# A gated cross-attention and expert-mix block: a quarter of the mix is added by GpSimd, with the engine orders laid out anew

## What is computed

```python
x = x + tanh(g_xattn) * xattn(layernorm(x), ctx, mask, Wq, bq, ..., Wo, bo)   # windows of 128 columns, 8 heads of 32
x = x + tanh(g_ffn)   * ffn(layernorm(x), router_weight, router_bias, expert_bias)

def ffn(h, ...):                              # h: rows by 2048
    scores = softmax(h @ router_weight.T + router_bias)        # 64 experts
    w = the 8 largest scores of a row, zero elsewhere          # rows by 64
    return h * w.sum(-1) + w @ expert_bias                     # the mix
```

## Time and profile before

| | |
|---|---|
| runs | 1418.84 us median of 3 (1418.77 to 1421.61) |
| profiled execution | 1415.67 us, span of the core 1413.9 us |
| TensorE busy | 1294.0 us, 92% of the span |
| VectorE busy | 1090.5 us, 77% |
| GpSimd busy | 1012.6 us, 72% |
| ScalarE busy | 794.7 us, 56% |
| DMA | 124.67 MB, mean 88 GB/s |
| chain of work that ended last | TensorE 70%, VectorE 19%, ScalarE 5%, issue 4%, GpSimd 1% |

### The profile page before, as it was taken

The page is one execution under the profiler, slowest core; times in us unless marked ns, Lnnn a source line. Parts: engine busy times, 40 slices in busy tenths (PEclk is TensorE's granted clock), DMA queues, the critical chain, the costliest instruction groups (busy, mean ns, idle before and its releaser), DMA issues.

```text
span 1413.9 us, 39778 instructions
## 1 busy us (share of the span) xinstructions
PE 1294.0 (92%) x16064; PEld 1158.8 (82%) x16064; DVE 1090.5 (77%) x1949; ACT 794.7 (56%) x1430; POOL 1012.6 (72%) x988
## 2 busy tenths in 40 slices
PE   1899999899989999899998999989998999989964
PEld 1898998789978899689986899878997889869953
DVE  6569668896679867897778966889677986786665
ACT  1455665655565566655556556665556555666534
POOL 4487887578867788578885788757885788856650
PEclk9999999999999999999999999999999999999976
DMA  8431111541127111361114511163112611132003
GB/s 251 114 107 46 41 44 43 180 131 43 42 65 242 48 40 46 118 188 47 44 40 136 173 47 41 41 209 100 48 45 83 216 47 47 46 122 59 23 5 119
DMA packets 129269, 124.67 MB, mean 88 GB/s; under 512 B 12352, under 2 KB 97472, under 8 KB 128448
## 3 DMA queue, kind: packets, MB, share of 16 engines
q1 hardware_dynamic: 129088, 122.14, 28.7%
HBM read 88.45 MB, written 33.65 MB: 86 GB/s over the span
## 4 chain that ended last, share of the span: by engine, by line
PE 70%; DVE 19%; ACT 5%; issue 4%; POOL 1%; DMA 1%; SPq 0%; DVEq 0%; ACTq 0%; POOLq 0%
PE ring L279 7%; PE ring L280 7%; PE ring L281 7%; PE ring L348 4%; PE ring L387 4%; DVE X L859 4%; PE ring L319 4%; PE ring L357 4%; PE ring L388 4%; PE ring L294 4%; PE ring L389 4%; PE ring L295 4%; PE ring L296 4%; PE ring L400 4%; PE ring L371 3%
## 5 line engine op out<-in xcount | busy, mean ns | idle before, releaser
L279 PE MATMUL ring<-z_hi,wqk_hi 128*128 128x256 f32 x1024 | 291.8, 285 | 30.0 <-POOL z_lo L986 30.0
L280 PE MATMUL ring<-z_hi,wqk_lo 128*128 128x256 f32 x1024 | 290.8, 284 | 0.0
L281 PE MATMUL ring<-z_lo,wqk_hi 128*128 128x256 f32 x1024 | 290.6, 284 | 0.0
L1002 POOL TENSOR_TENSOR X<-X,xt 128x512 f32<-128x512 f32 x128 | 165.7, 1300 | 145.7 <-DVE xt L764 140.6
L1018 POOL TENSOR_SCALAR hc<-X,ln 128x256 f32<-128x256 f32 x256 | 233.3, 928 | 0.5 <-POOL X L1002 0.5
L764 DVE SCALAR_TENSOR_TENSOR xt<-ring,cst,mg 128x256 f32<-128x256 f32 x256 | 112.1, 479 | 151.8 <-PE ring L389 151.8
L591 ACT ACTIVATE q<-ring,cst 128x256 f32<-128x256 f32 x64 | 30.3, 474 | 350.3 <-PE ring L281 350.3
L279 PEld LDWEIGHTS ring<-z_hi,wqk_hi 128*128 128x128 f32 x1024 | 197.2, 193 | 33.1 <-issue 30.6
L748 DVE RECIPROCAL o<-ring 128x512 f32<-128x512 f32 x64 | 214.3, 3348 | 0.5 <-PE ring L357 0.5
L992 POOL TENSOR_TENSOR cx_lo<-cx,cx_hi 128x512 fp32r<-128x512 f32 x128 | 168.6, 1317 | 48.6 <-ACT cx_hi L599 48.6
L280 PEld LDWEIGHTS ring<-z_hi,wqk_lo 128*128 128x128 f32 x1024 | 197.4, 193 | 2.5
(11 more groups left out here) (131 smaller groups left out, 3366.4 us busy)
## 6 DMA issues: line engine op xcount, KB each, us to landing
cx<-in_ctx SPq DMA_DIRECT2D x128, 256.0 KB, 2.9
out_y<-X SPq DMA_DIRECT2D x128, 256.0 KB, 2.7
X<-in_x SPq DMA_DIRECT2D x112, 256.0 KB, 5.8
mk<-in_mask SPq DMA_DIRECT2D x64, 128.0 KB, 3.2
mg<-in_mask SPq DMA_DIRECT2D x64, 128.0 KB, 3.2
X<-in_x SPq DMA_DIRECT2D x4, 1024.0 KB, 8.0
sel<-rows_d SPq DMA_DIRECT2D x256, 3.0 KB
X<-in_eb SPq DMA_DIRECT2D x2, 512.0 KB, 8.1
```

The lines of the kernel that those rows point to most:

```text
L279: e.matmul(o, wqk_hi[:, t, cols], z_hi[:, t, :], t == 0, False)
L280: e.matmul(o, wqk_lo[:, t, cols], z_hi[:, t, :], False, False)
L281: last = e.matmul(o, wqk_hi[:, t, cols], z_lo[:, t, :], False, t == DT - 1)
```

## The change

The first of the four column blocks of a row tile, `c = 0`, is now added by GpSimd. ScalarE writes it into a buffer of its own, `xp`, instead of `xm`. GpSimd multiplies the four tiles of X with `c = 0` by the row's scale in one go (`scale_x`, 4 instructions, once the scale is there and the statistics have read X), and later adds `xp` to each (`add_mix`). VectorE keeps the other 12 additions. `xp` is one buffer, so ScalarE waits for GpSimd's addition of the row tile before. The stores of a row tile go in the order c = 1, 2, 3, 0. The slots of all engines are new.

```diff
-    rows=-10.75, z32=-26, z_hi=-16.75, z_lo=-14.25, q=-11, q_ev=-9, k=-9, k_ev=-3.75, mk=-33.5, mkb=-25,
-    c_hi=-15, c_lo=-10.5, v=-10.5, v_ev=-7.25, v_gap=-0.75,
-    S=0.75, top=2.5, split=6, MT=9, mt_ev=8.75, ST=14.25, exp=16.5, DEN=18.25, PV=18.5, rc=19, on=21.25,
-    gelu=24.25, mg=5, ot_hi=24.75, ot_lo=29, WO=30.25, WO_gap=1.5, xt=32.25, x1=35.5, bn2=40,
-    h=39.5, hT=43.25, hT_gap=0.25, ht_hi=45.25, ht_lo=44.75, R=51.25,
-    norm2=29.5, L=34.75, LT=35.5, c_top=35, c_exp=36, c_w=42, wT=41.75, wt_hi=43.75, wt_lo=42.75, mix=45.25, m_gap=0.25,
-    m_ev=47.5, x2=47.25, rl=52.5, rl_gap=1,
-    x_1=0.5, x_gap=3.75, bn1=64.75, bn1_gap=1.25, norm1=95,
+    rows=-10.75, z32=-26, z_hi=-16.75, z_lo=-14.25, q=-10.25, q_ev=-8.25, k=-8.25, k_ev=-3, mk=-33.5, mkb=-25,
+    c_hi=-14.25, c_lo=-10.25, v=-9.75, v_ev=-6.5, v_gap=-0.75,
+    S=1.25, top=3.25, split=6.75, MT=9.75, mt_ev=10.5, ST=15, exp=17.25, DEN=19, PV=19.25, rc=19.75, on=22,
+    gelu=25, mg=5, ot_hi=28.5, ot_lo=29.75, WO=31, WO_gap=1.75, xt=33, x1=36.25, bn2=39.75,
+    h=40, hT=44, hT_gap=0.25, ht_hi=47, ht_lo=45.5, R=52,
+    norm2=30.25, L=36.25, LT=36.25, c_top=35.75, c_exp=36.75, c_w=42.75, wT=42.5, wt_hi=44.5, wt_lo=43.5, mix=46, m_gap=0.25,
+    sx=47.25, m_ev=48.25, x2=48.25, rl=56.5, rl_gap=1,
+    x_1=0.5, x_gap=3.75, bn1=68.75, bn1_gap=1.25, norm1=95,
...
+        xp = sb("xp", [128, 512])
...
             def store(b, t, c):
-                e.wait_ge(x2_v, (b * DT + t) * 4 + c + 1)
+                if c == 0:
+                    e.wait_ge(x2_g, b * DT + t + 1)
+                else:
+                    e.wait_ge(x2_v, (b * DT + t) * 3 + c)
...
-                        store(b, i // 4, i % 4)
+                        store(b, i // 4, (i + 1) % 4)
...
             def shift_mix(b, t, c):
                 i = (b * DT + t) * 4 + c
-                if i >= 2:
-                    e.wait_ge(x2_v, i - 1)
+                n = (b * DT + t) * 3 + c - 1
+                if c == 0 and i:
+                    e.wait_ge(x2_g, b * DT + t)
+                elif c and n >= 2:
+                    e.wait_ge(x2_v, n - 1)
                 e.wait_ge(mix_pe, i + 1)
                 if t == 0 and c == 0:
                     e.wait_ge(ac_v, b + 1)
-                e.activation(xm[i % 2][:], bank("mix", i)[:], ACT.Identity, bias=sc[:, t, 7:8]).then_inc(xm_a, 1)
+                to = xm[n % 2] if c else xp
+                e.activation(to[:], bank("mix", i)[:], ACT.Identity, bias=sc[:, t, 7:8]).then_inc(xm_a, 1)
...
                     for b in batch(t, C["x2"] + C["m_gap"] * i):
-                        add_mix(b, i // 4, i % 4)
+                        if i % 4:
+                            add_mix(b, i // 4, i % 4)
...
+            def add_mix(b, t):
+                xs = X[b % 2][:, t, 0:512]
+                e.wait_ge(sx_g, DT * b + t + 1)
+                e.wait_ge(xm_a, (b * DT + t) * 4 + 1)
+                e.tensor_tensor(xs, xs, xp[:], ALU.add).then_inc(x2_g, 1)
+
+            def scale_x(b):
+                e.wait_ge(bn2_v, 16 * (b + 1))
+                e.wait_ge(ac_v, b + 1)
+                for t in range(DT):
+                    xs = X[b % 2][:, t, 0:512]
+                    e.tensor_scalar(xs, xs, sc[:, t, 6:7], None, ALU.mult).then_inc(sx_g, 1)
...
+                for b in batch(t, C["sx"]):
+                    scale_x(b)
+                for k in range(DT):
+                    for b in batch(t, C["x2"] + C["m_gap"] * 4 * k):
+                        add_mix(b, k)
```

More of the change, by code:

```diff
@@ L192, in gated_block_kernel @@
             "L", "LT", "dm", "lg", "t8", "neg", "mr", "sel", "ex", "w2", "ac"))
-        wm_v, wT_pe, wthi_a, wtlo_v, mix_pe, xm_a, x2_v = (sem(n) for n in (
-            "wm", "wT", "wthi", "wtlo", "mix", "xm", "x2"))
+        wm_v, wT_pe, wthi_a, wtlo_v, mix_pe, xm_a, x2_v, sx_g, x2_g = (sem(n) for n in (
+            "wm", "wT", "wthi", "wtlo", "mix", "xm", "x2", "sx", "x2g"))
         TICKS = range(-32 * 8, 8 * (128 * (NB + 1) + 96))
@@ L813, in c_top @@
                 if b:
-                    e.wait_ge(x2_v, 16 * b)
+                    e.wait_ge(x2_v, 12 * b)
+                    e.wait_ge(x2_g, 4 * b)
                 e.wait_ge(t8_v, b + 1)
@@ L853, in add_mix @@
                 i = (b * DT + t) * 4 + c
+                n = (b * DT + t) * 3 + c - 1
                 xs = X[b % 2][:, t, c * 512:(c + 1) * 512]
-                if t == 0 and c == 0:
+                if t == 0 and c == 1:
                     e.wait_ge(h_g, NU * (b + 1))
@@ L858, in add_mix @@
                 e.wait_ge(xm_a, i + 1)
-                e.scalar_tensor_tensor(out=xs, in0=xs, scalar=sc[:, t, 6:7], in1=xm[i % 2][:], op0=ALU.mult, op1=ALU.add).then_inc(x2_v, 1)
+                e.scalar_tensor_tensor(out=xs, in0=xs, scalar=sc[:, t, 6:7], in1=xm[n % 2][:], op0=ALU.mult,
+                                       op1=ALU.add).then_inc(x2_v, 1)
             def input_stats(b, t, r):
```

## The result

The changed kernel takes 1440.69 us (median of 4 runs, 1438.53 to 1442.12), the kernel before 1418.8 us in the same session (4 runs, 1416.78 to 1421.61): 1.0155 times as long, interval 1.0137 to 1.0174. That is 22 us slower, and outside the predicted range. The profiled execution of the changed kernel took 1438.53 us with a span of 1436.7, against 1415.67 and 1413.9: 22.8 us of span to explain.

A forecast was written before the change was run, and what follows sets the result against it. TensorE, busy 92% of the span, was taken as the bound. Mix +1.4, statistics -5 and tail +2.6 gave -1.0 us: 1414.7 profiled, 1417.8 as median; own range 1414 to 1422, with rivals 1406 to 1429.

The forecast's parts named there:

- Step (5): Input statistics one unit after the mix: later slots bring k's evacuation earlier, -5 us over seven, bounds 0 and -7.
- Step (4): Mix of batch 0 walked through: q starts 0.2 us later a mix; seven mixes +1.4 us, bounds -7 to +10.
- rival B: After the mix: GpSimd's backlog ends last and TensorE's transposes wait for hc; at two microseconds more, 1425 us; chance 0.1.
- the order outside the mix: Engine orders and ring bank pattern else unchanged outside the mix, covered by VectorE's and GpSimd's slack: costed at nothing.
- (2): GpSimd's added work: four adds of 1.3 us and four scalings of 1.7 us, in all 12 us a batch.
- (7): Tail, with no TensorE work to hide under: groups of four additions take 3.45 us, +2.6 us.
- Plain units: Units away from the mix, where TensorE has no gap: claimed to still take 18.51 us.
- Rival A: In the mix, GpSimd's scalings lock VectorE too, holding each of the first two additions: +9.4, 1428 us; chance 0.2.
- D: Rival: z_lo does not hold VectorE's additions in its new place mid-mix: -30, 1389 us; chance 0.05.
- C: Rival: lock order falls well and scalings are short; mix -1.0, statistics -0.9, seven times: -11.5, 1407 us; chance 0.25.
- (1): VectorE loses 4 of 16 additions a batch: 30 us in all with lock waits, 24 clean.

The follow-up runs named there:

- e1: Changed kernel with the input statistics and the loads of x back in their old slots: 1436.1 us, ratio 1.0141 to the kernel before.
- e2: Kernel before with the changed kernel's new slots alone, VectorE making all 16 additions: 1410.15 us, ratio 0.9960.
- e7: Changed kernel with 18 extra matmuls (128x256) ahead of S in each mix, to keep TensorE busy: 1440.29 us, ratio 1.0169.
- e9: Code of e7 with GpSimd's fourth addition of every mix over 16 columns instead of 512: 1431.27 us, ratio 1.0097.
- e3: Changed kernel's code, work moved to GpSimd, with the slots of the kernel before: 1426.61 us, ratio 1.0075.
- e6: Changed kernel with GpSimd's additions of xp replaced by one-operation scalings of 384 columns: 1433.11 us, ratio 1.0115.
- e5: Changed kernel with each GpSimd scaling of X over 16 columns instead of 512: 1439.74 us, ratio 1.0161.
- e10: Changed kernel with z_lo moved ahead of GpSimd's four scalings and two xp buffers instead of one: 1442.38 us, ratio 1.0183.

## Why the prediction was wrong

**Step (5), the input statistics, failed, and is the largest error**: forecast -5 us with 0 as the worse bound, measured +12.0. It counted the statistics between reciprocal and split in the unit right behind the mix, and stopped there. It did not ask in which unit the last of the 16 would then stand. That unit has the four result statistics (L781) ahead of k; four input statistics came on top, and the unit went from 18.55 to 19.96. The unit looked at won nothing, as two statistics rather than one stood before its split and a small CAST was stretched to 1.68. e1 and e2 show both ways that the place of the statistics is the cause: the old place in the changed kernel brings 18.51 back, the new place in unmoved code brings 20.03.

**Step (4), the mix, ended its walk too early**: forecast +1.4 us with +10 as the worse bound, measured +9.3. The changed kernel reaches the mix 1.1 us later, so the walk is laid beside the trace from `w_turn`'s first matmul (243.57 before; 244.70 and 584.14 in batches 0 and 2 after):

```text
us from w_turn's first matmul     walked    batch 0 (clock fell)    batch 2 (clock kept)
GpSimd's add of t0 starts           8.8            8.5                     8.6
z_lo ends                          15.1           14.8                    14.8
maxima start                       21.8           20.1                    19.7
q starts                           25.5           25.3                    23.8
TensorE comes to hc                32.8           32.5                    31.2
hc ends                            31.9           32.1                    32.8
```

The walk of GpSimd holds within 0.4 us. The maxima came 1.8 earlier than walked, as no addition of GpSimd fell between VectorE's; the prediction had named that case and priced it at -0.9 to -0.3 a mix. Where the clock stays the long unit is indeed 0.9 shorter (30.8 against 31.7). That q in batch 0 came where it was forecast is luck: the fall of the clock, which the walk does not have, took back what the maxima won. And the sum closed at q. Behind it stands GpSimd's queue, which it put at nothing: 2.2 us a batch where the clock stays (20.85 against 18.67). So (4) had the lock between the engines right, and its failed term is the one that it left out.

**That queue is rival B**, given 0.1. Its text has hc ready 0.9 us before TensorE wants it; in batch 2 it is 1.6 to 1.7 behind. Of that error 1.7 us is TensorE, which comes sooner, and 0.8 is hc, which ends later (the fourth addition takes 1.83 instead of 1.3, and cx_lo and add_x behind it 1.85 and 1.73 instead of 1.3). e7 and e9 decide it: with the added matmuls hc is waited for in each batch and nothing is won; with the fourth addition cut as well, 11 us come back.

**Nor is +9.3 the cost of the move.** It is the sum of -16.2 for the order (e2) and +25.5 for the move on top of it; taken the other way round, of +6.2 for the move (e3) and +3.1 for the order on top. The prediction costed the order outside the mix at nothing and inside it by a few tenths; it saw that z_full comes ahead of add_x, but gave no price to z_full, in place of two tensor_tensor, standing beside the last additions. Of the move's 3.6 us a batch on that order, 0.3 are in the first unit, 1.1 in the long one while the clock stays up (30.8 against 29.7, mostly gone in e6), 2.1 in the unit behind it, and 1.6 of these hang on the fourth addition (e9).

**Right were**: (2) the scalings, 1.67 us each in the mean, forecast 1.7. (7) the tail, +2.0 from the last mark, forecast +2.6, the groups 3.27 us each instead of 3.45. Plain units still take 18.51 (18.47 to 18.51 in the mean). Rival A is refuted in its place, since the first two additions beside the scalings took 1.85 us together, and in its price, since shorter scalings gain nothing (e5). D is refuted too: z_lo does hold additions in the middle. C's sign was right for the order alone, for another reason. (1) was wrong in size: the additions of VectorE fell from 128 to 96, yet their time only from 114.6 to 109.2 us, as each became longer. The groups of the changed kernel that answer to the earlier trace rows and give the scalings' price:

```profile
L869 DVE SCALAR_TENSOR_TENSOR X<-X,sc,xm 128x512 f32<-128x512 f32 x96 | 109.2, 1168 | 19.1 <-ACT xm L672 18.8
...
L1031 POOL TENSOR_SCALAR X<-X,sc 128x512 f32<-128x512 f32 x32 | 52.9, 1670 | 9.2 <-DVE sc L852 9.2
```

The Trainium skill (SBUF — State Buffer, "Who interferes with whom") would have the four scalings hold the first additions of VectorE whole. The trace does not agree: two additions beside them took 1.85 us together, where two with GpSimd idle take 1.54. For z_lo and the additions of GpSimd it agrees, in the 6.51 us for four.

The 0.3 us a batch of the first unit go with one small instruction: the first tensor_scalar of `c_top` (L825, 128x4) takes 0.49 us in batches 1 to 6 of the changed kernel, of e3 and of e6, and 0.17 in their batches 0 and 7 and in all of the kernel before and e2; `w_turn` then waits 0.3 longer. Why it is longer is open. Open are also the 2.5 us of the third statistics unit and the 0.6 us that the unit behind the mix keeps in e9. That the fourth addition done by VectorE again, with the rest of the move kept, would bring the same as cutting it short was not tried.

## What to carry to other kernels

When a block of work is moved in a hand-laid order, follow it to its last instruction and ask what that unit already holds; the unit where the block begins tells nothing of it. Test a new order and the work moved within it apart: here one was worth -4.6 us of span and the other +27.4, and the prediction forecast only the sum. Walk a later repetition as well as the first: batch 0 showed none of the loss. Before giving work to an engine with 47% idle in a window, look at what it must deliver right after that window, and count its queue from the last input it has to wait for, since shortening what lies ahead of that wait gains nothing.

## What the hardware showed unexpectedly

- Behind idle stretches of the same length the granted clock fell in some mixes and not in others. In the changed kernel it fell behind the two waits of 0.86 and 1.44 us, 0.2 us apart, in four of seven mixes, and behind the single wait of 1.88 for the weights in two of them. In e10 it fell behind a single wait of 2.00 us in six of seven. In the kernel before the single wait of 2.42 left it at 1.00, and so did one of 1.97 to 1.98 in five mixes; the same wait in the last mix did not. That is this line, and the window behind it; the long unit took 33.29 us there instead of 31.70:

```profile
1267.92 1.94 PE L357 MATMUL ring<-P,ones 128*32 128x512 f32 x8 [1.97 <-DVE mx L727]
```

```profile
1267.50:1271.50 4.00, 3.58 (x41) 1.90 (x42) 4.00 (x7) 1.18 (x2) 4.00 (x7) 0.57 0.27 98
```

  What tells these cases apart the runs do not say.
- A tensor_scalar of GpSimd with two operations can be the one that gives way: z_full took 5.18 us beside VectorE's additions instead of 2.16, and four of those 3.62 (3.1 with GpSimd idle, by the earlier trace rows). Beside a tensor_tensor of GpSimd the additions take 1.6 us each, and the tensor_tensor of 512 columns 1.7 instead of 1.3.
- Operations of VectorE over 16 columns, 0.2 us alone, took 1.68 (CAST, L748) and 1.23 us (L750) beside GpSimd's tensor_tensor.
